# Edge loop on TensorE: the order of the one-hot sums and the second variance within a step

## The reference, cut to what matters

```python
e     = LN(silu(edge_attr @ emb_W0 + emb_b0) @ emb_W1 + emb_b1) * emb_g + emb_b
e_in  = concat([e, mesh_nfeat[src], grid_nfeat[dst]])
e_new = LN(silu(e_in @ edge_W0 + edge_b0) @ edge_W1 + edge_b1) * edge_g + edge_beta + e
agg   = segment_sum(e_new, dst)
```

## Time and profile before

| what | value |
|---|---|
| median of three runs | 2416.91 us |
| the profiled execution's own time | 2417.75 us |
| its span (first to last instruction) | 2416.0 us |
| busy over the span: PE, PEld | 92%, 78% |
| busy over the span: DVE, ACT, POOL | 61%, 50%, 46% |
| granted TensorE clock, mean of the span | 0.972 of full speed |
| stretch of the edge loop (steps with n from 0 to 175) | about 800 to 2290 us |

### The profile page before, as it was taken

The page is one execution under the profiler, slowest core; times in us unless marked ns, Lnnn a source line. Parts: engine busy times, 40 slices in busy tenths (PEclk is TensorE's granted clock), DMA queues, the critical chain, the costliest instruction groups (busy, mean ns, idle before and its releaser), DMA issues. The chain is left out here.

```text
span 2416.0 us, 44677 instructions
## 1 busy us (share of the span) xinstructions
PE 2222.8 (92%) x13057; PEld 1886.8 (78%) x13060; DVE 1475.7 (61%) x3258; ACT 1217.5 (50%) x2255; POOL 1120.9 (46%) x1665
## 2 busy tenths in 40 slices
PE   2989499999987799999999999999999999999797
PEld 1436388777765698898989988898898989889676
DVE  7012299534362567766677677766767677766566
ACT  0121111324321667666776766766767766667421
POOL 4777700000000455655556556555555556555323
PEclk9999799999998899999999999999999999999899
DMA  6223100000022532332323332332233333223121
GB/s 192 80 48 88 12 8 0 36 5 35 26 88 97 156 64 61 65 64 59 63 61 65 65 61 62 64 65 61 61 65 61 65 61 66 60 61 64 25 92 43
DMA packets 76276, 149.66 MB, mean 62 GB/s; under 512 B 14689, under 2 KB 15789, under 8 KB 76219
## 3 DMA queue, kind: packets, MB, share of 16 engines
q0 software_dynamic: 44864, 93.18, 19.7%
q1 hardware_dynamic: 31243, 55.63, 6.9%
q10 hardware_dynamic: 112, 0.11, 0.0%
HBM read 129.12 MB, written 19.46 MB: 61 GB/s over the span
## 5 line engine op out<-in xcount | busy, mean ns | idle before, releaser
L1180 POOL DMA_INDIRECT c_from_src<-s_dst_table,c_at_nodes x176 | 298.0, 1693 | 32.1 <-issue 32.1
L1529 PE MATMUL c_edge_bank<-c_m_hi,c_pt_hi 128*128 128x512 f32 x704 | 294.2, 418 | 0.0
L1303 DVE CUSTOM_DVE_ANT_0 c_var_bank<-c_var_bank,c_p,k_floor 128x512 f32<-128x512 f32 x176 | 132.4, 752 | 250.9 <-PE c_var_bank L1474 250.0
L1530 PE MATMUL c_edge_bank<-c_m_lo,c_pt_hi 128*128 128x512 f32 x704 | 279.6, 397 | 0.0
L1531 PE MATMUL c_edge_bank<-c_m_hi,c_pt_lo 128*128 128x512 f32 x704 | 278.4, 395 | 0.0
L1174 POOL DMA_INDIRECT c_from_src<-s_mesh_table,c_at_nodes x176 | 202.1, 1148 | 152.1 <-POOL c_at_nodes L1170 142.8
L1186 POOL TENSOR_TENSOR c_dev<-c_var,k_half 128x1 f32<-128x1 f32 x176 | 97.8, 556 | 319.2 <-DVE c_var L1287 319.2
L1417 ACT ACTIVATE c_h<-c_from_src 128x512 f32<-128x512 f32 x176 | 111.3, 633 | 265.2 <-DVE c_from_src L1322 265.2
L321 POOL DMA_INDIRECT s_records<-a_stage_rec,a_stage_row x170 | 207.6, 1221 | 56.8 <-issue 48.8
L1472 PE MATMUL c_var_bank<-c_m_hi,c_pt_hi 128*128 128x384 f32 x704 | 224.8, 319 | 7.8 <-ACT c_var_bank L1391 5.3
L1472 PE MATMUL c_var_bank<-c_m_hi,c_ht_hi 128*128 128x384 f32 x704 | 221.5, 315 | 4.9 <-DVE c_ht_lo L1292 4.6
(11 more groups left out here) (314 smaller groups left out, 5981.5 us busy)
## 6 DMA issues: line engine op xcount, KB each, us to landing
k_w<-in_L_gnn_Ws_self_dram SPq DMA_DIRECT2D x3, 1024.0 KB, 10.7
k_w<-in_L_gnn_Ws_neigh_dram SPq DMA_DIRECT2D x3, 1024.0 KB, 13.1
c_from_src<-s_mesh_table,c_at_nodes POOLq DMA_INDIRECT x176, 3.5
c_from_src<-s_dst_table,c_at_nodes POOLq DMA_INDIRECT x176, 4.7
s_records<-a_stage_rec,a_stage_row POOLq DMA_INDIRECT x170, 2.6
a_mesh<-in_L_gnn_mesh_nfeat_dram SPq DMA_DIRECT2D x10, 250.0 KB
k_h<-in_x_dram SPq DMA_DIRECT2D x1, 2500.0 KB
s_mesh_table<-a_mesh_out SPq DMA_DIRECT2D x10, 250.0 KB
```

The source lines that it names most:

```text
L1180: pool.indirect_dma_start(from_src[u][:], None, scratch["dst_table"], bass.IndirectOffsetOnAxis(ap=at_nodes[u][:, 1:2], axis=0), compute_o ...
L1303: dve.tensor_tensor_reduce(var1_bank[:], var1_bank[:], p[u % 2][:], 1.0 / D, k["floor"][:, 0:1], ALU.mult, ALU.add, var[u][:, 0:1]).then_i ...
L1529: pe.matmul(edge_bank[:], left[0], m_hi[1][:, c, :], start=False, stop=False, skip_group_check=True)
L1530: pe.matmul(edge_bank[:], left[0], m_lo[1][:, c, :], start=False, stop=False, skip_group_check=True)
```

## The change

In each step of PE's queue the sums of n-2 stand ahead of the second variance of n-1. In the last lines of the phase (L1554 to L1557) that order was there already for the last two tiles and stays. One wait is added inside `sums`, ahead of its last matmul: that matmul writes into turn_bank, which may still hold h of tile n-1 (turned in the same step), until DVE's low_ht has read it. In the old order `variance2` had waited for that before the sums came.

```diff
@@ sums(n, u)
             for bank, part in ((sum_p_bank, rp_hi[u]), (sum_p_bank, rp_lo[u]), (sum_h_bank, rh_hi[u % 2]), (sum_h_bank, rh_lo[u % 2])):
                 pe.matmul(bank[:], hot[u][:], part[:], start=False, stop=False, skip_group_check=True)
             need(pe, sum_now_ok, n)
+            pe.wait_ge(ht_lo_ok, n + 2 if not isinstance(n, int) else min(n + 2, TILES))
             pe.matmul(tile_r, hot[u][:], dev_parts[u][:], start=True, stop=True, skip_group_check=True).then_inc(sums_mm, 1)
@@ step(i, v, u)
                 turn_stack(i + 1)
+            if exists(n - 2):
+                sums(n - 2, (u - 2) % 4)
             if exists(n - 1):
                 variance2(n - 1, (u - 1) % 4)
-            if exists(n - 2):
-                sums(n - 2, (u - 2) % 4)
```

## The result

The changed kernel takes 2685.53 us (median of 4 runs, 2683.35 to 2688.07), the kernel before 2417.41 us beside it (2412.22 to 2419.03): a ratio of 1.1114, 95% interval 1.1093 to 1.1134. The prediction was 2682. The span of the profiled execution grew from 2416.0 to 2685.3 us.

The account below looks back on a forecast made before the run. The prediction took PE, busy 298.91 of 300 us in the edge loop, as the bound. It summed 2417.75 us + 251 (regular steps) + 14 (bucket ends) = 2683, or 2682 against the median, range 2580 to 2750.

Parts of the forecast that it names:

- What bounds the kernel: Edge loop: PE, busy 298.91 of 300 us, sets the pace; almost no waits to release, the largest 4.6 us.
- Part 1: Sums in their new place: each step loses 0.94 us plus PE's lead, 4.53 us for four tiles.
- Part 2: Second variance ending later delays DVE and ACT: four tiles lose 5.77 us instead of 4.53, 251 us over 174 steps.
- Part 3: Nine places where a bucket is left: hot 2.1 us later, 19 us, less 4.6 of old waits; net +14.
- rival C: Edge loop: PE's pauses lower its clock; half the loop at 1.2 GHz gives some 3380 us; chance 0.03.
- clock 1.00 throughout: Sign expected in the profile after: PE's granted clock stays at 1.00; a fall inside the loop would refute the forecast.
- Costed at nothing: Added wait on ht_lo, POOL's later dev1 and sums finished 1.8 us earlier: claimed to cost nothing.
- The stall itself is the cover: Longer steps hide POOL's later dev1; without the stall h would be late by under 1 us, fourth step alone.
- A: Rival: DVE and ACT don't fall further behind in the loop; 197 us there, 2628 in all; chance 0.12.
- B: Rival: register load ahead of the wait on hot, or overlapping; 61 us lost, 2479 in all; chance 0.06.
- D: Rival: not slower, sums fill PE's wait for ht_lo at bucket ends; gives back 4.6 us, 2412; chance 0.02.

Follow-up runs that it names:

- Experiment 1: The changed kernel with the register load of the bucket number moved ahead of the wait on hot: 2563.61 us, 1.0607 of the kernel before.
- experiment 2: The changed kernel with a second register load of the same number right behind the first, its value unused: 2818.96 us, 1.1663 of the kernel before.
- experiment 3: The kernel before (old order) with a second register load of the same number behind the first: 2438.55 us, 1.0087.
- Experiment 5: The changed kernel with DVE adding up and leaving tile n-2 ahead of the second variance's reduction of step n: 2622.28 us, 1.0852 of the kernel before.
- experiment 4: The changed kernel with hot made one step before its use and the rh waits only before the matmuls that read it: 2502.92 us, 1.0353.
- experiment 6: The changed kernel with hot early, later waits on rh, and adding and leaving ahead of the second variance's reduction: 2465.76 us, 1.0199 of the kernel before.
- experiment 10: The kernel before (old order) with hot made early and POOL's gather issued behind dev1: 2408.67 us, 0.9969.
- experiment 7: The kernel before (old order) with hot made early and the later waits on rh alone: 2416.47 us, 0.9995.

## Why the prediction was right, point by point

**What bounds the kernel.** Right: a pause of PE is time, and nothing waited that the new order could release.

**Part 1, the sums wait for hot and then for the register load.** Right in kind and size. From hot's end to the weights load I took 0.84 us, the profile after has 0.83 (and 0.84 at the bucket end at 1160 us). Experiment 1 took the load out of the way and won 122 us (129 expected), experiment 2 doubled it, experiment 3 showed it hidden in the old order.

**Part 2, the late second variance.** Right. In the first step L1303 starts 2.85 us in (1435.69 less 1432.84; predicted 2.84) and hot ends at 5.93 (5.99). In the third, hot ends at 6.22 (6.20), and turn_h waits for attr_t 0.6 us, in 41 groups. The steps lost 1.67, 0.98, 2.00 and 1.10 us (first to fourth) against predicted 1.72, 1.06, 1.93 and 1.06: 5.75 instead of 5.77 for four tiles, 250 us in 43.5 groups. That the prediction took the fourth step before as 8.6 us and not 8.47 did no harm, since it added up losses and not lengths. Experiment 5 removed the part and gave 2622 where 2627 stood.

**Part 3, where a bucket is left.** Right in sign, and nearly right in sum by luck. 268 us less 250 leaves 18 us outside the regular groups, where I had 14, but the terms are others. By the starts of POOL's build_stack, the 41 groups of four tiles after the first take 34 us more than 41 regular ones in the changed kernel (I had 19) and 13 us more in the kernel before (I had 4.6, the waits alone; PE also loses time as it starts again). The difference is 21 us, and some 3 the other way lie outside these groups. The 34 us hold two things: the pause, which was foreseen, and its consequence for the clock, which was not. At the two bucket ends where the clock stayed at 1.00 the group is 2.2 and 1.9 us longer (2.1 predicted), at the other seven 3.2 to 4.9. PE's timeline and the windows at one of the seven:

```profile
1160.84 0.79 PE L1500 MATMUL c_sum_p_bank<-c_rp_hi,c_hot 128*128 128x512 f32 x1 [3.90 <-DVE c_rp_lo L1317]
1161.43 0.63 PE L1500 MATMUL c_sum_p_bank<-c_rp_lo,c_hot 128*128 128x512 f32 x1
...
1173.08 0.39 PE L1500 MATMUL c_sum_p_bank<-c_rp_lo,c_hot 128*128 128x512 f32 x1
```

```profile
1150.00:1158.00 8.00, 6.95 (x41) 5.87 (x39) 5.79 (x15) 3.77 (x7) 3.10 (x7) 1.00 0.32 69
1158.00:1162.00 4.00, 1.16 (x3) 0.97 (x4) 3.23 (x6) 1.74 (x4) 2.28 (x2) 0.64 0.25 48
1162.00:1166.00 4.00, 4.00 (x16) 3.81 (x15) 0.00 (x0) 0.38 (x1) 0.00 (x0) 0.51 0.17 30
1166.00:1170.00 4.00, 4.00 (x28) 3.75 (x28) 2.67 (x8) 3.36 (x7) 1.12 (x4) 1.00 0.00 0
```

Within a pause of 3.90 us the granted clock falls, and behind it is 0.51, the lower of the two levels; the sums' matmul takes 0.63 us instead of 0.39, and by 1166 the clock is back at 1.00. About 5 us of PE's work (1160.84 to 1166) were done at half rate, so some 2.6 us were lost there, and by the estimate of experiment 2 17 us at all seven. My rival C described this for the whole loop; it holds at seven of the nine bucket ends (in windows of 20 us from 860 us to the loop's end) and nowhere else there, and my own sign "clock 1.00 throughout" failed. The length of one pause doesn't decide it: behind 3.03 us (to 993.10) and 2.70 us (to 2017.09) the clock stayed at 1.00, behind another 2.70 us (to 1499.74) it fell, and so it did at the bucket end at 1328 us, where one step has pauses of 1.47 and 1.25 us. The regular pauses of 0.6 to 1.3 us left the clock alone: in 1150 to 1158 it was 1.00.

**Costed at nothing.** The added wait on ht_lo does not appear as a wait ahead of L1503 in any view; taking it out would be a race, so that was not tried. "The stall itself is the cover" was right, and so was about the price without it, under 1 us once in four steps: experiment 4 shows 0.95 us, experiment 6 48 us or 1.1 a group. The way there was not the one I named: it is add_r and turn_h in the one, ACT's hidden layer ahead of feature_rows in the other, and not a late h in the fourth step. And I left this price out of what I expected of experiments 4 and 6, which is the miss of both.

**The rivals.** A (2628) fell by the unequal steps, B (2479) by the 0.83 us behind hot, C but for the bucket ends, D altogether.

## What to carry to other kernels

Work moved forward in an in-order queue takes its waits with it, and what the queue itself has to do behind such a wait (here a register load) becomes visible: put a load that needs no late data ahead of the wait (122 us of 268 here). Read, for each engine, what stands behind the thing that now ends later; here one late reduction came back as a wait of a transpose and a later hot (63 us, with the copies and the clock at bucket ends). And when a stall is removed, look for the ring that it had covered, before concluding that the order is to blame.

## What the runs showed that I had not expected

A single pause of 3.9 us on PE halved its granted clock for the next 5 us or so, where 0.6 to 1.3 us in every step did not; in between it went both ways, with falls behind 1.9 us (experiment 2) and none behind 3.03. The second register load cost 0.65 us a step in a regular group although its own record is 0.3 us long. And in the kernel before, where PE was already busy 99% of the loop and waited for 7.6 us in all from 860 to 2250 us, hot early together with POOL's gather behind dev1 gave 8 us (2408.67, 0.9969 with 0.9958 to 0.9980). POOL's build_stack, once in four steps, dates it: first and last of its 41 starts in the window 840 to 2250 us, for the kernel before and for experiment 10:

```profile
L1158 POOL CAST c_attr_hi<-k_recs x41: 194/198/198, 863.9 to 2200.0; 128x16 fp32r x40, 128x16 fp32r<-128x16 f32 x1
```

```profile
L1158 POOL CAST c_attr_hi<-k_recs x41: 197/197/199, 860.1 to 2193.5; 128x16 fp32r x40, 128x16 fp32r<-128x16 f32 x1
```

Of the 9.9 us between the two spans (2416.0 and 2406.1) 3.8 are there by the loop's first steps, 2.7 come in the 160 steps between, and 3.4 behind the last. So most of it lies at the loop's two ends and not in its steady state. At the start 3.0 us are there before the first step: PE's first turn_stack of the phase comes at 785.59 us instead of 788.59, behind the same wait of 8.50 us for a transfer. In the three kernels with POOL's edit it comes at 785.0 to 785.6 us, in the nine others at 786.6 to 789.2; why is open. At the end PE's waits ahead of the sums of the last two tiles are 4.4 us instead of 7.5. That goes with the early hot: experiment 7 has 4.5 us there, and loses about as much in the loop as it wins behind it.
